# The seam between two chunks of a routed expert layer: other waits on VectorE, another order on TensorE and ScalarE

## The chip, the cores and the metric

The kernel runs on one core of a Trainium2 chip. The metric is device time in microseconds (us) of one execution; the number compared is the median of several executions. Engines are named as in the profile: PE is TensorE (PEld its weight loads), DVE is VectorE, ACT is ScalarE, POOL is GpSimd, SP is SyncE, whose queue issues most transfers.

## The reference

The input is 16 x 256 = 4096 tokens of width 128. Three residual layers follow each other: half a routed feed-forward layer, an attention without softmax over positions, and half the same feed-forward layer again.

```python
x = x + 0.5 * ffn(layernorm(x))     # first pass
x = x + attention(layernorm(x))
x = x + 0.5 * ffn(layernorm(x))     # second pass
# ffn: rmsnorm, 32 experts, 4 chosen per token
g = t @ gate_w.T + gate_b
vals, idx = top_k(g, 4); w = softmax(vals)
h1 = einsum('th,efh->tef', t, w1) + b1
h = min(h1[..., ::2], 7) * sigmoid(1.702 * glu) * (clip(h1[..., 1::2], -7, 7) + 1)
out = einsum('tef,ehf->th', h * combine, w2) + combine @ b2
```

## The kernel before, in words

The tokens are cut into two chunks of 16 tiles of 128 tokens (NCHUNK = 2, CT = 16). For each chunk a router finds four experts per token. POOL then writes the normalised rows into a DRAM array `xs[c]`, sorted by expert, with 64 indirect transfers (L539, one for each tile and choice). The sorted rows make 24 **groups** of 512 slots per chunk (NG = 24), padded so that every 128 slots have one expert. The function `experts(f)` works through the 48 groups of both chunks (NGF = 48), in the first pass (f = 0) and in the second (f = 1). SP stores what comes out to `ys[c]`, and POOL gathers it back per token with 64 indirect transfers per chunk (L564); VectorE adds the gathered rows to `X`.

For group n the steps are these, each on one engine:

- SP loads 512 rows into `xrow[n % 2]` (L356, 256 KB).
- PE turns them, `turn_rows(n)`, four transposes into a PSUM bank (L1214, from `xrow`); ACT copies the bank to `xT` (`copy_rows`, L639).
- PE makes `first_product(n)` (L1311); DVE clips its two halves (`glu`, L1005, and `lin`, L1010), ACT makes `swish` (L631), and DVE makes `hid` (L1018).
- PE turns that, `turn_hid(n)` (L1214, from `hid`), into the bank `HT`; ACT copies it to `hidT` (`copy_hid`, L634).
- PE makes `second_product(n)` into the bank `YP` (L1320); ACT copies it to `yrow` (`copy_y`, L626), and SP stores that (L361, 256 KB).

All buffers come in twos by n % 2, and `YP` and `HT` are one bank each. The engines run in software pipelines whose order is written out by hand. In step k PE does `turn_rows(k)`, `turn_hid(k-3)`, `first_product(k-1)` and `second_product(k-4)`, ACT `copy_y(k-5)`, `swish(k-2)`, `copy_hid(k-3)` and `copy_rows(k)`, and DVE `glu`, `lin` and `hid` of group k-1. An engine runs its instructions in order, so a wait holds up all that stands behind it.

**The seam** is the place where chunk 0 ends and chunk 1 begins, groups 21 to 25. The rows of group 24 can only be loaded once all 64 scatters of chunk 1 have landed (semaphore `scattered[1]`), and that is late. So PE and ACT have a function `seam()` for steps 24 to 26, in which the second products are spread out, counted by semaphores of its own (`seam_turned` for the three `turn_hid`, `seam_multiplied` for the four second products). VectorE has none: at step k it makes `hid(k-1)` after a wait for `turned >= k + 1` (L1016 and L1017), which in a usual step says that `turn_hid(k-3)` has read the buffer that `hid(k-1)` will overwrite. In the seam `turned` counts the `turn_rows` of groups 24, 25 and 26.

SP's queue around the seam, in order: store 18, wait for `scattered[1]`, load 24, load 25, stores 19 and 20, load 26, store 21, load 27, store 22, load 28, store 23 (L352 to L382). Load k waits for `turned` of step k-2. POOL's first gather of chunk 0 waits for all 24 stores of chunk 0 and, by the pacing in `keep_to_experts`, for the copy `copy_hid(24)`; from there on a gather is issued about every third of a step. The first gather of chunk 1 waits for the stores of groups 24 to 47. VectorE has one loop up to group step 27 (COMB_A = 28) and from there another, in which it also adds gathered tiles.

Of the kernel before, what the change touches and what calls it, by code (L numbers as in the profile page):

```python
# [25 lines left out]
NG = ST // GT  # L26
# [12 lines left out]
NGF = NCHUNK * NG  # L39
# [35 lines left out]
def live(k, lag, n):  # L75

    return not isinstance(k, int) or 0 <= k - lag < n
# [8 lines left out]
def build(nc, x, wq, bq, wk, bk, wvT, bv, wfqT, bfq, wfkT, bfk,  # L86
          nscale, gwT, gate_b, w12T, b1, b2, out, xs, ys):
    with ExitStack() as ctx:  # L88
# [489 lines left out]
        def _(act):  # L578
# [42 lines left out]
            def experts(f):  # L621
# [11 lines left out]
                def copy_hid(n, r):  # L633
                    a.activation(hidT[:, r, :], HT, ACT.Copy).then_inc(hidT_ready, 1)  # L634
# [19 lines left out]
                def seam():  # L654
# [9 lines left out]
                    copy_y(k - 4, 0, m - 2, YP)  # L664
                    swish_of(k - 1, 1)
                    act.wait_ge(seam_multiplied, y + 2)
                    copy_y(k - 3, 1, m - 2, YP)
                    act.wait_ge(seam_turned, z + 2)
                    copy_hid(k - 2, 0)
                    copy_rows(k, 0)  # L670
# [108 lines left out]
        def _(dve):  # L779
# [209 lines left out]
            def experts(f):  # L989
# [3 lines left out]
                def step(k, r, adding=None):  # L993
# [19 lines left out]
                    if live(k, 1, NGF):  # L1013
                        dve.wait_ge(swish_ready, k + g0)
                        dve.wait_ge(lin_ready, k + g0)
                        if live(k, 3, NGF):  # L1016
                            dve.wait_ge(turned, k + (t0 + 1))  # L1017
                        v.scalar_tensor_tensor(hid[:, s, :], lin[:, s, :], 1.0, swish[:, s, :], ALU.add, ALU.mult)\  # L1018
                            .then_inc(hid_ready, 1)
# [7 lines left out]
                for k in range(4):  # L1027
                    step(k, k % 2)
                with dve.Fori(0, (COMB_A - 4) // 4) as i:
                    for j in range(4):  # L1030
                        step(i * 4 + (4 + j), j % 2)
                with dve.Fori(0, CTA // 2) as i:
                    for j in range(4):
                        step(i * 4 + (COMB_A + j), j % 2, Combine(i * 2 + j // 2, j // 2, i, 0, f) if j % 2 else None)
# [174 lines left out]
        def _(pe):  # L1209
# [74 lines left out]
            def experts(f):  # L1284
# [50 lines left out]
                def seam():  # L1335
                    k = NG
                    turn_hid(k - 3, 1).then_inc(seam_turned, 1)
                    first_product(k - 1, 1).then_inc(multiplied, 1)
                    second_product(k - 4, 0, YP, k - 4).then_inc(seam_multiplied, 1)
                    turn_rows(k, 0, k // 2).then_inc(turned, 1)  # L1340
                    second_product(k - 3, 1, YP, k - 3).then_inc(seam_multiplied, 1)
                    turn_hid(k - 2, 0).then_inc(seam_turned, 1)
                    turn_rows(k + 1, 1, k // 2).then_inc(turned, 1)
# [181 lines left out]
```

## Time and profile before

| What | Value |
| --- | --- |
| median of 3 executions | 724.93 us (724.14 to 725.18) |
| span of the profiled execution | 722.9 us |
| PE busy | 531.0 us, 73% |
| POOL busy | 506.2 us, 70% |
| DVE busy | 436.2 us, 60% |
| ACT busy | 347.2 us, 48% |
| POOL gathers (L564) on the chain that ended last | 8% of the span |

The span runs from the first to the last instruction of the profiled execution; no time of that execution beside its span was recorded. The median of the timed executions stands 2.0 us above the span, which is what lies around the instructions, and differences between executions. The kernel's stages lie in the span so: front and first router up to about 114 us, experts of the first pass up to 291 us, attention and the second router up to 460 us, experts of the second pass up to 634 us, and the last gathers and additions up to the end. Busy shares are averages over these stages; whether a wait costs time is read from the place where it lies.

### The profile page before, as it was taken

To read this page: it belongs to the slowest core of one execution; us is meant where nothing else is said; L and a number is where in the kernel's file an instruction comes from. 1 tells how busy PE (TensorE), PEld (TensorE's weight loads), DVE (VectorE), ACT (ScalarE), POOL (GpSimd) and SP (SyncE) were. 2 spreads that over 40 slices of the span, in tenths; PEclk is the share of its full clock that TensorE was granted. 3 is DMA by queue.
4 is the path that set the end of the run, shared out by engine and by line. 5 is a ranking of instruction groups with operands and counts; after the bars stand their busy time and mean duration, and the time that the engine had idled before them with its cause. 6 is when DMAs were issued, how large, how long until landed. Compare 5 with 4: busy or idle time off the path is not lost. (4 is left out here: it accounts for less than half of the span.)

```text
span 722.9 us, 12843 instructions
## 1 busy us (share of the span) xinstructions
PE 531.0 (73%) x3252; PEld 443.8 (61%) x3253; DVE 436.2 (60%) x1243; ACT 347.2 (48%) x752; POOL 506.2 (70%) x551
## 2 busy tenths in 40 slices
PE   6258879999899999385607854999999999933000
PEld 3154366999899998253504553699998999833000
DVE  6889233555547778378993868255564767845222
ACT  4444413666556666495606644366665666610000
POOL 3677777777527777777677777777752777767765
PEclk9556999999999999797557955999999999977555
DMA  7997115566546664222111111456655666524222
GB/s 271 392 375 289 52 54 153 197 194 200 175 147 197 199 210 154 81 54 53 48 52 54 51 52 55 138 182 208 203 168 177 201 198 206 160 78 128 66 62 58
DMA packets 56493, 108.28 MB, mean 150 GB/s; under 512 B 12576, under 2 KB 19968, under 8 KB 56320
## 3 DMA queue, kind: packets, MB, share of 16 engines
q1 hardware_dynamic: 40064, 74.13, 30.7%
q0 software_dynamic: 16384, 33.59, 16.1%
q8 instruction: 23, 0.38, 0.2%
q14 instruction: 22, 0.18, 0.1%
HBM read 51.00 MB, written 56.62 MB: 149 GB/s over the span
## 5 line engine op out<-in xcount | busy, mean ns | idle before, releaser
L564 POOL DMA_INDIRECT YG<-ys,row x256 | 245.0, 957 | 116.9 <-issue 75.4
L539 POOL DMA_INDIRECT xs<-U,row x256 | 250.7, 979 | 81.9 <-issue 74.6
L1311 PE MATMUL PS<-W,xT 128*128 x768 | 182.2, 380 | 0.2
L1311 PEld LDWEIGHTS PS<-W,xT 128*128 128x128 f32 x768 | 138.4, 190 | 16.1 <-issue 1.2
L1005 DVE TENSOR_SCALAR glulin<-PS 128x512 f32<-128x512 f32 x96 | 66.3, 691 | 127.8 <-PE PS L1320 84.3
L626 ACT ACTIVATE yrow<-PS 128x512 f32<-128x512 f32 x96 | 57.3, 597 | 103.3 <-PE PS L1320 103.3
L1320 PEld LDWEIGHTS PS<-W,hidT 128*128 128x128 f32 x768 | 100.7, 193 | 7.8 <-issue 3.4
L1320 PE MATMUL PS<-W,hidT 128*128 x768 | 102.8, 277 | 1.6 <-issue 1.2
L1018 DVE SCALAR_TENSOR_TENSOR hid<-glulin,swish 128x512 f32<-128x512 f32 x96 | 66.6, 694 | 16.0 <-ACT swish L631 10.5
L631 ACT ACTIVATE swish<-glulin 128x512 f32<-128x512 f32 x96 | 60.4, 629 | 30.5 <-DVE glulin L1005 26.7
L639 ACT ACTIVATE xT<-PS 128x512 f32<-128x512 f32 x96 | 56.3, 589 | 38.8 <-PE PS L1214 38.7
L1010 DVE TENSOR_SCALAR glulin<-PS 128x512 f32<-128x512 f32 x96 | 65.3, 680 | 0.0
L1214 PE MATMUL PS<-ident,xrow 128*128 128x128 f32 x384 | 58.5, 275 | 3.9 <-DMA xrow<-xs 3.8
L1214 PE MATMUL PS<-ident,hid 128*128 128x128 f32 x384 | 58.1, 274 | 1.9 <-ACT hidT L634 1.9
L634 ACT ACTIVATE hidT<-PS 128x512 f32<-128x512 f32 x96 | 55.6, 579 | 0.9 <-PE PS L1214 0.9
L1214 PEld LDWEIGHTS PS<-ident,xrow 128*128 128x128 f32 x384 | 45.4, 142 | 7.3 <-DMA xrow<-xs 6.5
L1214 PEld LDWEIGHTS PS<-ident,hid 128*128 128x128 f32 x384 | 45.2, 141 | 2.3 <-DVE hid L1018 2.3
L1063 DVE SCALAR_TENSOR_TENSOR PS<-YG,wtop,X 128x128 f32<-128x128 f32 x40 | 12.4, 353 | 50.5 <-issue 44.5
L981 DVE SCALAR_TENSOR_TENSOR X<-YG,wtop,X (+1 forms) x96 | 32.8, 341 | 3.9 <-DMA YG<-ys,row 3.9
L1214 PE MATMUL PS<-ident,U 128*128 128x128 f32 x64 | 14.5, 386 | 24.7 <-ACT U L595 24.7
L1231 PEld LDWEIGHTS PS<-gw,xT 128*128 128x128 f32 x128 | 25.8, 296 | 6.0 <-issue 3.6
L583 ACT ACTIVATE vq<-vq 128x32 f32<-128x32 f32 x6 | 1.4, 229 | 58.2 <-DVE vq L808 58.2
(178 smaller groups left out, 714.2 us busy)
## 6 DMA issues: line engine op xcount, KB each, us to landing
xrow<-xs SPq DMA_DIRECT2D x96, 256.0 KB
ys<-yrow SPq DMA_DIRECT2D x96, 256.0 KB
xs<-YG SPq DMA_DIRECT2D x6, 2048.0 KB, 13.7
W<-in_w12T SPq DMA_DIRECT2D x1, 6144.0 KB, 33.5
xs<-U,row POOLq DMA_INDIRECT x256
YG<-ys,row POOLq DMA_INDIRECT x256, 2.5
out<-X SPq DMA_DIRECT2D x7, 256.0 KB, 2.6
X<-in_x SPq DMA_DIRECT2D x4, 256.0 KB, 3.6
```

Source lines behind the costliest of these rows:

```text
L539: pool.indirect_dma_start(out=xs[c], out_offset=bass.IndirectOffsetOnAxis(ap=row[:, i:i + 1], axis=0), in_=U[:, (c * CT + t) * H:(c * CT + ...
L564: pool.indirect_dma_start(out=YG[:, t * TOPK + k, :], out_offset=None, in_=ys[c], in_offset=bass.IndirectOffsetOnAxis(ap=row[:, i:i + 1], ...
L626: a.activation(yrow[:, r, :], bank, ACT.Copy).then_inc(yrow_ready, 1)
L631: a.activation(swish[:, r, :], glu[:, r, :], ACT.Gelu_apprx_sigmoid).then_inc(swish_ready, 1)
L634: a.activation(hidT[:, r, :], HT, ACT.Copy).then_inc(hidT_ready, 1)
L639: a.activation(xT[:, r, :], TP[r], ACT.Copy, bias=1.0).then_inc(xT_ready, 1)
L1005: v.tensor_scalar(glu[:, s, :].rearrange("p (q f) -> p q f", q=GT), h1[:, 0], LIMIT, None, ALU.min).then_inc(glu_ready, 1)
L1010: v.tensor_scalar(lin[:, s, :].rearrange("p (q f) -> p q f", q=GT), h1[:, 1], -LIMIT, LIMIT, ALU.max, ALU.min).then_inc(lin_ready, 1)
L1018: v.scalar_tensor_tensor(hid[:, s, :], lin[:, s, :], 1.0, swish[:, s, :], ALU.add, ALU.mult)\
L1214: last = te.transpose(dst[:, q * P:(q + 1) * P], src[:, q * H:(q + 1) * H], ident[:])
L1311: last = te.matmul(h1, xT[:, r, q * P:(q + 1) * P], W[:, bass.ds(es[q], 2 * H)], start=True, stop=True)
L1320: last = te.matmul(bank[:, q * H:(q + 1) * H], hidT[:, r, q * P:(q + 1) * P], W[:, bass.ds(es[q] + 2 * H, H)], start=True, stop=True)
```

## The change

It has three parts. First, in PE's `seam()` the instructions `turn_hid(22)` and `second_product(21)` stand before `turn_rows(24)`; before, `turn_rows(24)` stood first, then `second_product(21)` and `turn_hid(22)`. Second, in ACT's `seam()` `copy_hid(22)` stands before `copy_y(21)`. Third, VectorE's `hid` of groups 23, 24 and 25 waits for `seam_turned` (1, 2 and 3 in its pass), which counts `turn_hid(21)`, `turn_hid(22)` and `turn_hid(23)`, and no longer for `turned`. For that VectorE's loop ends at step 23, and steps 24 to 27 are written out. Nothing is added or left out of the computation, and POOL and SP have the same instructions in the same order.

```diff
--- before.py
+++ after.py
@@ -663,10 +663,10 @@
                     act.wait_ge(seam_multiplied, y + 1)
                     copy_y(k - 4, 0, m - 2, YP)
                     swish_of(k - 1, 1)
+                    act.wait_ge(seam_turned, z + 2)
+                    copy_hid(k - 2, 0)
                     act.wait_ge(seam_multiplied, y + 2)
                     copy_y(k - 3, 1, m - 2, YP)
-                    act.wait_ge(seam_turned, z + 2)
-                    copy_hid(k - 2, 0)
                     copy_rows(k, 0)
                     copy_rows(k + 1, 1)
                     act.wait_ge(seam_multiplied, y + 3)
@@ -1013,7 +1013,9 @@
                     if live(k, 1, NGF):
                         dve.wait_ge(swish_ready, k + g0)
                         dve.wait_ge(lin_ready, k + g0)
-                        if live(k, 3, NGF):
+                        if isinstance(k, int) and NG <= k < NG + 3:
+                            dve.wait_ge(seam_turned, 3 * f + k - NG + 1)
+                        elif live(k, 3, NGF):
                             dve.wait_ge(turned, k + (t0 + 1))
                         v.scalar_tensor_tensor(hid[:, s, :], lin[:, s, :], 1.0, swish[:, s, :], ALU.add, ALU.mult)\
                             .then_inc(hid_ready, 1)
@@ -1026,9 +1028,11 @@
                 dve.wait_ge(base_done, CT * (f * NCHUNK + 1))
                 for k in range(4):
                     step(k, k % 2)
-                with dve.Fori(0, (COMB_A - 4) // 4) as i:
+                with dve.Fori(0, (NG - 4) // 4) as i:
                     for j in range(4):
                         step(i * 4 + (4 + j), j % 2)
+                for k in range(NG, COMB_A):
+                    step(k, k % 2)
                 with dve.Fori(0, CTA // 2) as i:
                     for j in range(4):
                         step(i * 4 + (COMB_A + j), j % 2, Combine(i * 2 + j // 2, j // 2, i, 0, f) if j % 2 else None)
@@ -1337,9 +1341,9 @@
                     turn_hid(k - 3, 1).then_inc(seam_turned, 1)
                     first_product(k - 1, 1).then_inc(multiplied, 1)
                     second_product(k - 4, 0, YP, k - 4).then_inc(seam_multiplied, 1)
+                    turn_hid(k - 2, 0).then_inc(seam_turned, 1)
+                    second_product(k - 3, 1, YP, k - 3).then_inc(seam_multiplied, 1)
                     turn_rows(k, 0, k // 2).then_inc(turned, 1)
-                    second_product(k - 3, 1, YP, k - 3).then_inc(seam_multiplied, 1)
-                    turn_hid(k - 2, 0).then_inc(seam_turned, 1)
                     turn_rows(k + 1, 1, k // 2).then_inc(turned, 1)
                     second_product(k - 2, 0, YP, k - 2).then_inc(seam_multiplied, 1)
                     turn_hid(k - 1, 1).then_inc(seam_turned, 1)
```

PE in the first pass's seam, from the end of `second_product(20)` on (`ident,xrow` is `turn_rows`, `ident,hid` is `turn_hid`, `W,hidT` a second product, whose four matmuls are four rows, of which the first stands; L1320 before is L1324 now). Before:

```order
L1214 MATMUL PS<-ident,xrow 128x128 [waits xT_ready,xrow_loaded0]
L1214 MATMUL PS<-ident,xrow 128x128 x3
L1289 TENSOR_LOAD eid
L1320 ISA [waits yrow_ready,hidT_ready]
L1320 MATMUL PS<-W,hidT 128x128
...
L1214 MATMUL PS<-ident,hid 128x128 [waits hidT_ready,hid_ready]
L1214 MATMUL PS<-ident,hid 128x128 x3
L1214 MATMUL PS<-ident,xrow 128x128 [waits xT_ready,xrow_loaded1]
L1214 MATMUL PS<-ident,xrow 128x128 x3
```

The same place in the change:

```order
L1218 MATMUL PS<-ident,hid 128x128 [waits hidT_ready,hid_ready]
L1218 MATMUL PS<-ident,hid 128x128 x3
L1293 TENSOR_LOAD eid
L1324 ISA [waits yrow_ready,hidT_ready]
L1324 MATMUL PS<-W,hidT 128x128
...
L1218 MATMUL PS<-ident,xrow 128x128 [waits xT_ready,xrow_loaded0]
L1218 MATMUL PS<-ident,xrow 128x128 x3
L1218 MATMUL PS<-ident,xrow 128x128 [waits xT_ready,xrow_loaded1]
L1218 MATMUL PS<-ident,xrow 128x128 x3
```

The two turns of chunk 1's rows now stand together behind the work of chunk 0; what follows them (`second_product(22)`, `turn_hid(23)`, `first_product(24)`) is as before.

VectorE at the end of its first loop, in the change (L1005 is `glu`, L1010 `lin`, L1020 `hid`):

```order
L1031 COMPARE_AND_BRANCH
L1005 TENSOR_SCALAR glulin<-PS 128x512 [waits swish_ready,multiplied]
L1010 TENSOR_SCALAR glulin<-PS 128x512 [waits hid_ready]
L1020 SCALAR_TENSOR_TENSOR hid<-glulin,swish 128x512 [waits seam_turned,lin_ready,swish_ready]
...
L1020 SCALAR_TENSOR_TENSOR hid<-glulin,swish 128x512 [waits turned,lin_ready,swish_ready]
L1036 UNCONDITIONAL_BRANCH
```

Before, these four steps were the last turn of the loop, and each `hid` waited for `turned`. Now three of them wait for `seam_turned`, and the fourth for `turned` as it did.

## Rows read from the trace of the kernel before

**Rows 1.** The waits of POOL: line waited for: us in total, times, longest us

```profile
POOL YG L564 <- issue: 75.4, 229, 2.2
POOL xs L539 <- issue: 74.6, 232, 4.2
```

**Rows 2.** POOL's timeline: start, duration, instruction, [idle before <- releaser]

```profile
210.94 0.97 POOL L564 DMA_INDIRECT YG<-ys,row  x1 [17.62 <-ACT hidT L634]
...
293.47 0.94 POOL L564 DMA_INDIRECT YG<-ys,row  x1 [1.02 <-issue]
...
554.38 0.97 POOL L564 DMA_INDIRECT YG<-ys,row  x1 [16.22 <-DMA ys<-yrow]
...
636.69 0.94 POOL L564 DMA_INDIRECT YG<-ys,row  x1 [1.57 <-issue]
```

**Rows 3.** One usual step of TensorE, from the timeline of all engines

```profile
184.47 1.05 PE L1320 MATMUL PS<-W,hidT 128*128 x8
...
185.36 0.60 PE L1214 MATMUL PS<-ident,xrow 128*128 128x128 f32 x4
...
186.24 1.89 PE L1311 MATMUL PS<-W,xT 128*128 x8
```

**Rows 4.** The first pass's seam, from the timeline of all engines

```profile
194.51 1.05 PE L1320 MATMUL PS<-W,hidT 128*128 x8
...
195.48 1.09 SPq L361 DMA_DIRECT2D ys<-yrow  x2
...
195.60 0.60 ACT L626 ACTIVATE yrow<-PS 128x512 f32<-128x512 f32 x1 [1.22 <-PE PS L1320]
...
197.36 0.65 PE L1214 MATMUL PS<-ident,xrow 128*128 128x128 f32 x4 [1.79 <-DMA xrow<-xs]
...
198.05 0.69 DVE L1018 SCALAR_TENSOR_TENSOR hid<-glulin,swish 128x512 f32<-128x512 f32 x1 [1.96 <-PE PS L1214]
...
203.25 1.89 PE L1311 MATMUL PS<-W,xT 128*128 x8
...
209.50 0.58 ACT L634 ACTIVATE hidT<-PS 128x512 f32<-128x512 f32 x1
```

**Rows 5.** The second pass's seam, from the timeline of all engines

```profile
540.32 2.45 SPq L361 DMA_DIRECT2D ys<-yrow  x2
...
540.71 1.05 PE L1320 MATMUL PS<-W,hidT 128*128 x8
...
541.80 0.60 ACT L626 ACTIVATE yrow<-PS 128x512 f32<-128x512 f32 x1 [1.22 <-PE PS L1320]
...
542.27 0.66 PE L1214 MATMUL PS<-ident,xrow 128*128 128x128 f32 x4 [0.51 <-DMA xrow<-xs]
...
542.88 1.15 PE L1320 MATMUL PS<-W,hidT 128*128 x8
...
546.72 1.89 PE L1311 MATMUL PS<-W,xT 128*128 x8
```

**Rows 6.** Windows: stretch, length, PE, PEld, DVE, ACT, POOL busy, PEclk, DMA, GB/s

```profile
194.00:196.00 2.00, 1.57 (x12) 1.30 (x10) 1.89 (x3) 0.78 (x2) 0.00 (x0) 1.00 0.31 40
196.00:197.36 1.36, 0.00 (x1) 0.00 (x1) 0.09 (x1) 0.72 (x2) 0.00 (x0) 1.00 0.84 283
197.36:198.50 1.14, 0.90 (x6) 0.66 (x7) 0.45 (x1) 0.00 (x0) 0.00 (x0) 1.00 1.03 395
198.50:200.00 1.50, 1.50 (x11) 1.50 (x11) 0.24 (x1) 0.25 (x1) 0.00 (x0) 0.65 0.80 197
200.00:201.50 1.50, 1.50 (x8) 1.18 (x6) 0.00 (x0) 1.24 (x3) 0.00 (x0) 0.50 0.39 150
```

**Rows 7.** Windows, the second pass's seam, columns as above

```profile
543.80:545.00 1.20, 1.10 (x11) 0.86 (x9) 0.00 (x0) 0.94 (x2) 0.00 (x0) 1.00 0.90 222
```

**Rows 8.** The page's DMA issues, median us to landing last

```profile
out<-X SPq DMA_DIRECT2D x7, 256.0 KB, 2.6
```

**Rows 9.** VectorE where it enters its next loop, from the timeline

```profile
214.63 0.69 DVE L1005 TENSOR_SCALAR glulin<-PS 128x512 f32<-128x512 f32 x1 [1.41 <-PE PS L1320]
```

## The prediction

> **What bounds the kernel now.** I read the waits first, for the engine that never rests. POOL waited 229 and 232 times for nothing but its own issue before a gather or a scatter, and nearly all these waits are of 0.3 us [rows 1]: it sends transfer after transfer. POOL's timeline then shows where it does rest [rows 2]. In each pass it waits once for long, between the last scatter of chunk 1 and the first gather of chunk 0: 17.62 us up to 210.94, and 16.22 us up to 554.38. From 210.94 the chain is tight up to the next long wait (64 gathers bring it to 293.47, where it waits 1.02 us instead of 0.3 for the last stores; then gathers and scatters of the attention stage), and from 554.38 up to 636.69, where the wait is 1.57 us, again for the last stores. So the kernel's length is POOL's chain plus two rests, and each rest ends with the experts' work on PE, ACT and DVE. What ends the first rest is the copy of `hid` 24, which starts at 209.50 and takes 0.58 us [rows 4]: 0.86 us later the gather starts. Store 23 comes at nearly the same time. Both lie some steps behind `first_product(24)`, so the question is when that product starts.
>
> The timeline of the two seams answers it. In the first pass PE ends `second_product(20)` at 195.56, has nothing for 1.79 us until the rows of chunk 1 are in (197.36), and only then goes on with work of chunk 0 that needed no rows [rows 4]. `hid` 23 on DVE sits 1.96 us in the same wait and starts at 198.05. `first_product(24)` starts at 203.25. In the second pass the rows are in at 542.27, PE had waited 0.51 us, and the product starts at 546.72 [rows 5]: 4.45 us after the rows against 5.89 us in the first. The windows tell why: in the first pass the granted clock is 0.65 and then 0.50, that is the 1.2 GHz level, from about 199 us on, behind PE's idle 1.79 us [rows 6]; in the second, with shorter idle times, it is 1.00 [rows 7].
>
> **The change part by part.** No instruction is added or dropped; the sum is about starts. The spacings on PE are those of a usual step [rows 3]: a turn starts 0.89 us after a second product does, and two turns take 0.88 us, so 0.44 each.
>
> First pass. `turn_hid(22)` starts at 194.51 + 0.89 = 195.40, since `hid` 22 is long made. `second_product(21)` must wait until ACT has emptied the bank YP: copy of y 20 from 195.60 to 196.20 [rows 4], so it starts at about 196.33 and ends at 197.38. Both turns of rows then start at 197.36 and 197.80; the rows' arrival is not changed, as SP's and POOL's orders stay. ACT has copied `hid` 22 by 197.3. Next it must copy y 21, and here is **the next wait**: the buffer `yrow[1]` is free only when store 19 has landed, and behind this copy on ACT stand both `copy_rows`, on PE `second_product(22)`. Store 19 was issued at 195.48 as third of four transfers of 262 KB. The windows moved 80, 385 and 450 KB up to 196, 197.36 and 198.5 [rows 6]; the third transfer ends at 786 KB, so at 197.36 + 321/395 = 198.17, and with some 0.2 us for its notice, an estimate, it is free at 198.4. ACT copies until 199.0, `second_product(22)` starts at 199.1, `turn_hid(23)` at 200.0 and `first_product(24)` at 200.45. ACT copies the rows of group 24 by about 199.6, so they are not late, and `hid` 23, made by 197.6 behind its `swish`, isn't either. That is 203.25 - 200.45 = **2.8 us earlier**, of which some 1.4 us is the clock, taken as kept: PE's idle pieces are now 0.33 and about 0.7 us, and pieces of 0.51 us and less went with 1.00 in the second pass. The bounds of the landing: an `out` store of the same size lands 2.6 us after issue [rows 8], 198.1, which gives 3.1 us; if it doesn't bind at all, PE's spacing gives 3.7; a landing at 199.2 gives 2.0. I take 2.8 because the four transfers share the queue, which the `out` stores don't.
> The Trainium skill ("DMA: Bandwidth & Descriptors", section "Anatomy of one DMA") gives a DMA, measured there on GpSimd's path, as 2.0 us plus its bytes at 436 GB/s. That makes 2.6 us here, as the `out` row does, and the gain would be 3.1 us by it.
>
> Second pass. `second_product(21)` waits for the copy of y 20, over at 542.40 [rows 5], and starts at 542.48. The turns follow at 543.37 and 543.81. That is 1.1 us later than the first turn before; what hangs on it, load 26, has over 3 us until PE wants it. Store 19, issued at 540.32, is in at 543.2 by the 2.9 us of above, before y 21 is ready (543.53). Then `second_product(22)` starts at 544.25, `turn_hid(23)` at 545.14, `first_product(24)` at 545.58, against 546.72: 1.14 us. A second product behind idle time took 0.61 us to start instead of 0.44 [rows 5], so I take **1.05 us**, with 0.5 to 1.2 as bounds.
>
> What ends the rests follows: behind `first_product(24)` all stands as before, so the copy of `hid` 24 and store 23 move by the same amounts, and POOL's two chains with them. The last stores of each pass come as much earlier, as PE's steady steps aren't touched; both sides of the waits at 293.47 and 636.69 move together. Attention and router start from these and move as a block. VectorE's unrolled steps cost nothing: the same twelve operations, and their cover is DVE's idle time of over 1 us a step. The sum is 2.8 + 1.05 = 3.85 us. Against the profiled execution it is 722.9 - 3.85 = 719.05 of span; with the 2.0 us that the median stands above the span, 724.93 - 3.85 = **721.1 us**.
>
> **The rivals.** My forecast (A) has 0.66.
> B, *the clock falls all the same* in the first seam, behind the two smaller idle pieces: half speed costs at least 1.5 x 0.35 + 1.5 x 0.5 = 1.3 us by the two windows [rows 6], so 1.4 + 1.05 remain, 722.5 us. For it: PE is still not full there. Against it: the second pass. 0.12.
> C, *ACT is the new bound*: stores 19 and 20 land after 199.5 since the queue is full at 395 GB/s, and ACT, standing in order, holds the rows' copies. The first gain falls to about 1.7 us and the second to 0.6: 722.6 us. 0.08.
> D, *no change*: POOL's first gather hangs on something that the product doesn't move, such as a store behind loads on SP, and only some tenths pass through: 724.3 us. The row at 554.38 names a store's landing as its releaser, which speaks for it; that store too waits for `turn_rows(26)` and y 23, which move. 0.09.
> E, *slower*: VectorE's code. It now leaves its loop right in the seam and enters the next from straight code; if its instructions aren't there, DVE stands at one such place in each pass. The trace's longest wait named issue before a repeated transfer is 4.2 us, the next 2.2 [rows 1]; at 4.2 on the path of each pass the kernel ends at 721.1 + 8.4 = 729.5 us. It decides from 1.9 us per pass on. Against it: before, VectorE entered its next loop at 214.63 with 1.41 us idle, all of it named as waiting for PE [rows 9], and at the new exit `hid` 23 has 2.4 us to spare. 0.05.
> The Trainium skill ("Runtime: NRT & Kernel Launch", section "Instruction fetch mechanics") says that a taken branch whose target is not in the two pages at hand stalls until it is fetched. The trace shows no such stall on VectorE at its present loop entry.
>
> **How the numbers follow.** About 0.2%, 1.45 us, is what a measurement of this kernel can tell from no change. A, B and C lie beyond it: faster 0.86. D is within: same 0.09. E: slower 0.05. The range runs from A with a store that doesn't bind (a gain of 3.7 + 1.2 and some tenths of scatter: 719.8) up to B and C with as much scatter, 722.9; it leaves out D, E and the edges.
>
> **What would show it.** In the changed profile: `turn_hid(22)` some 2 us before the first turn of chunk 1's rows; `hid` 23 at about 196.9, no longer released by PE; the rows still turned at about 197.4; the copy of y 21 on ACT with a wait for a DMA; `first_product(24)` near 200.4 and a clock of 1.00 from 198.5 to 203; the first gather near 208.1, and POOL's rests at 14.8 and 15.2 us instead of 17.6 and 16.2. I am wrong if the gathers don't start earlier although the product does, if the wait at 293.47 or 636.69 grows by what the first gather gained, or if the clock is 0.50 in the seam.

## The result, and the profile after

The change is slower: 725.25 us against 723.48 us (22 executions of each), ratio 1.0022 with a 95% interval of 1.0015 to 1.0029, 1.8 us by the medians, where 3.85 us less (721.1 us) were forecast. The profiled execution went from 722.9 to 724.9 us of span.

GpSimd's timeline, the changed kernel, the rows that answer to [rows 2] (start, duration, instruction, idle before and its releaser):

```profile
208.98 0.98 POOL L564 DMA_INDIRECT YG<-ys,row  x1 [15.61 <-ACT hidT L634]
...
291.54 0.95 POOL L564 DMA_INDIRECT YG<-ys,row  x1 [1.17 <-issue]
...
556.10 0.97 POOL L564 DMA_INDIRECT YG<-ys,row  x1 [17.16 <-ACT hidT L634]
...
638.71 0.94 POOL L564 DMA_INDIRECT YG<-ys,row  x1 [1.87 <-issue]
```

The first gather comes 1.96 us earlier, and at 291.54 POOL is still 1.93 us ahead of [rows 2]. At 556.10 it is 1.72 us behind, at 638.71 it is 2.02 us behind, and that is the end's difference. So the first seam gained, and between 291 and 556 us 3.65 us were lost.

**The first seam**, from the timeline of the changed kernel (L1324 is the second product, L1315 the first, L1218 the turns), beside [rows 4]:

```profile
195.53 2.35 SPq L361 DMA_DIRECT2D ys<-yrow  x2
...
195.82 1.05 PE L1324 MATMUL PS<-W,hidT 128*128 x8
...
197.76 1.15 PE L1324 MATMUL PS<-W,hidT 128*128 x8 [0.44 <-ACT yrow L626]
...
198.06 0.69 DVE L1020 SCALAR_TENSOR_TENSOR hid<-glulin,swish 128x512 f32<-128x512 f32 x1 [0.75 <-ACT swish L631]
...
198.75 1.04 PE L1218 MATMUL PS<-ident,xrow 128*128 128x128 f32 x8
199.01 0.60 ACT L626 ACTIVATE yrow<-PS 128x512 f32<-128x512 f32 x1 [0.49 <-DMA ys<-yrow]
...
201.28 1.89 PE L1315 MATMUL PS<-W,xT 128*128 x8
```

Each step is the forecast one. PE goes through chunk 0's work without waiting for rows, `hid` 23 waits for its `swish` and no longer for PE, ACT waits 0.49 us for store 19, and the granted clock stays at 1.00, the 2.4 GHz level (windows from 194.0 to 201.5). The product comes 1.97 us earlier than at 203.25, not 2.8. Two things hold ACT's copy of `y` 21 back to the same moment, and either alone would have done it. Store 19, issued at 195.53, lets the copy start only at 199.01, 3.48 us later, where the forecast took 2.9. And PE reaches the seam 1.3 us later in this execution (195.82 against 194.51), so that `y` 21 itself was ready at about 198.95 (an estimate: the copy of `y` 22 starts 1.19 us after its product does). PE's lateness began at the first turn of the pass, at 115.18 against 114.09, ahead of anything that the change touches.

**The second seam**, same view, beside [rows 5]:

```profile
540.90 1.15 PE L1324 MATMUL PS<-W,hidT 128*128 x8 [0.44 <-ACT yrow L626]
...
541.10 0.90 SPq L361 DMA_DIRECT2D ys<-yrow  x2
...
542.89 0.66 PE L1218 MATMUL PS<-ident,xrow 128*128 128x128 f32 x4 [0.84 <-DMA xrow<-xs]
...
544.70 0.60 ACT L626 ACTIVATE yrow<-PS 128x512 f32<-128x512 f32 x1 [3.04 <-DMA ys<-yrow]
...
545.54 2.07 PE L1324 MATMUL PS<-W,hidT 128*128 x8 [0.90 <-ACT yrow L626]
...
548.25 2.08 PE L1315 MATMUL PS<-W,xT 128*128 x8
```

Here the change's own order puts `second_product(21)` at 540.90. By the same 1.19 us `y` 21 was ready at about 542.1, but ACT may copy it only when store 19, issued at 541.10 behind the loads, has landed: it idles 3.04 us before 544.70, some 2.6 of them with `y` 21 ready. The store took 3.6 us. PE stands behind ACT and its clock falls, as the windows of the changed kernel show (columns as in [rows 6]):

```profile
543.00:544.50 1.50, 1.07 (x8) 0.73 (x8) 0.00 (x0) 0.00 (x0) 0.00 (x0) 1.00 1.01 388
544.50:546.00 1.50, 0.60 (x4) 0.47 (x3) 0.00 (x0) 1.30 (x3) 0.00 (x0) 0.74 0.69 209
546.00:548.00 2.00, 2.00 (x11) 2.00 (x11) 0.00 (x0) 0.63 (x2) 0.00 (x0) 0.50 0.84 252
```

**The scatters between the seams.** The 64 scatters of chunk 1 in the second pass began 1.57 us earlier than before (454.79 against 456.36) and ended 0.78 us later (538.94 against 538.16). They took 2.35 us more, in a stretch in which POOL's program is unchanged. The page's groups of the changed kernel say which transfer it was; before, the mean of L539 was 979 ns:

```profile
L564 POOL DMA_INDIRECT YG<-ys,row x256 | 245.1, 958 | 116.2 <-issue 74.9
L539 POOL DMA_INDIRECT xs<-U,row x256 | 253.2, 989 | 81.8 <-issue 74.5
```

A mean of 989 ns hides two kinds: nearly all scatters take 0.96 us, and 8 of these 64 take 1.27 to 1.46 us. Before, 2 of the 64 were so long. That is the sum: 1.57 us ahead, less 2.35 us of long scatters, less 0.94 us of a longer rest (17.16 against 16.22 us) is 1.72 us behind.

**When a scatter is long.** The changed kernel's timeline, one long scatter, and one of the kernel before:

```profile
500.13 0.69 DVE L1020 SCALAR_TENSOR_TENSOR hid<-glulin,swish 128x512 f32<-128x512 f32 x1 [0.18 <-ACT swish L631]
500.26 1.39 POOL L539 DMA_INDIRECT xs<-U,row  x1 [0.30 <-issue]
```

```profile
505.38 0.96 POOL L539 DMA_INDIRECT xs<-U,row  x1 [0.30 <-issue]
505.40 0.70 DVE L1018 SCALAR_TENSOR_TENSOR hid<-glulin,swish 128x512 f32<-128x512 f32 x1
```

VectorE's `hid` just ahead of the scatter makes it long; just behind, it does nothing, and `hid` itself takes 0.69 us in both. Take all scatters of the experts' stages in nine traces with `lin` in SBUF (the two above and `r1`, `r2`, `n`, `e7`, `e5`, `e8b` and `e9b` below) and the `hid` before each. Where `hid` started 0.05 to 0.40 us before the scatter, 109 of 110 were held (1.17 to 1.48 us, the longest where `hid` started last); the one exception, 0.96 us, lies at the edge of 0.05. Where it started 0.4 to 0.6 us before, the mean was 1.02 us. Everywhere else all took 0.95 to 0.97 us. However late the scatter starts in that stretch, it ends some 1.52 us after `hid` started, about 0.83 us after `hid` ended.

The gathers are held in the same way, though there are fewer meetings: in the nine traces 67 of 67 gathers that began 0.05 to 0.40 us after a `hid` took 1.11 to 1.44 us instead of 0.94. One of them, from the change:

```profile
213.93 0.69 DVE L1020 SCALAR_TENSOR_TENSOR hid<-glulin,swish 128x512 f32<-128x512 f32 x1 [0.19 <-ACT swish L631]
214.02 1.42 POOL L564 DMA_INDIRECT YG<-ys,row  x1 [0.30 <-issue]
```

The Trainium skill ("SBUF — State Buffer", section "Who interferes with whom") says that a VectorE operation with two inputs in SBUF contends with GpSimd operations that read SBUF, for a shared pair of ports that one holds for its whole instruction, and that issue order decides who waits. The traces agree for the transfer that starts second, at 0.45 us an encounter. They do not for `hid`, which takes 0.68 to 0.73 us in all 656 cases where it starts during a transfer of POOL. The same section infers that such an operation leaves the making of a DMA's descriptors alone; these indirect transfers are held all the same, and which part of them is held no run here shows.

### The profile page after: what moved, and what is told of

Same layout as the page of the kernel before. It is cut to its first block and busy times, and to the rows that moved or that the text cites. A ratio compares the mean times of both kernels' runs of the same rounds, so it can differ in the third digit from the quotient of the medians.

```text
span 724.9 us, 12826 instructions
## 1 busy us (share of the span) xinstructions
PE 533.5 (74%) x3252; PEld 446.9 (62%) x3253; DVE 436.2 (60%) x1243; ACT 347.6 (48%) x752; POOL 508.9 (70%) x551
## 3 DMA queue, kind: packets, MB, share of 16 engines
q0 software_dynamic: 16384, 33.59, 16.4%
## 5 line engine op out<-in xcount | busy, mean ns | idle before, releaser
L539 POOL DMA_INDIRECT xs<-U,row x256 | 253.2, 989 | 81.8 <-issue 74.5
L1315 PE MATMUL PS<-W,xT 128*128 x768 | 182.4, 380 | 0.1
L1315 PEld LDWEIGHTS PS<-W,xT 128*128 128x128 f32 x768 | 138.7, 191 | 16.0 <-issue 1.0
L1005 DVE TENSOR_SCALAR glulin<-PS 128x512 f32<-128x512 f32 x96 | 66.4, 691 | 130.7 <-PE PS L1324 84.4
L1324 PEld LDWEIGHTS PS<-W,hidT 128*128 128x128 f32 x768 | 100.8, 193 | 9.0 <-issue 4.6
L1324 PE MATMUL PS<-W,hidT 128*128 x768 | 102.9, 277 | 2.8 <-ACT yrow L626 1.8
L1020 DVE SCALAR_TENSOR_TENSOR hid<-glulin,swish 128x512 f32<-128x512 f32 x96 | 66.6, 694 | 14.8 <-ACT swish L631 11.9
L1010 DVE TENSOR_SCALAR glulin<-PS 128x512 f32<-128x512 f32 x96 | 65.4, 681 | 0.0
L1218 PE MATMUL PS<-ident,xrow 128*128 128x128 f32 x384 | 57.9, 274 | 4.1 <-DMA xrow<-xs 4.0
L1218 PE MATMUL PS<-ident,hid 128*128 128x128 f32 x384 | 58.1, 274 | 2.0 <-ACT hidT L634 2.0
L1218 PEld LDWEIGHTS PS<-ident,xrow 128*128 128x128 f32 x384 | 45.0, 141 | 7.6 <-DMA xrow<-xs 6.8
L1218 PEld LDWEIGHTS PS<-ident,hid 128*128 128x128 f32 x384 | 45.2, 141 | 2.3 <-DVE hid L1020 2.3
L1218 PE MATMUL PS<-ident,U 128*128 128x128 f32 x64 | 14.6, 388 | 24.6 <-ACT U L595 24.6
L1235 PEld LDWEIGHTS PS<-gw,xT 128*128 128x128 f32 x128 | 27.5, 313 | 6.1 <-issue 3.7
L1235 PE MATMUL PS<-gw,xT 128*128 128x32 f32 x128 | 27.5, 376 | 4.0 <-DVE topi L845 3.0
```

What stands on the lines that cost most here:

```text
L539: pool.indirect_dma_start(out=xs[c], out_offset=bass.IndirectOffsetOnAxis(ap=row[:, i:i + 1], axis=0), in_=U[:, (c * CT + t) * H:(c * CT + ...
L1005: v.tensor_scalar(glu[:, s, :].rearrange("p (q f) -> p q f", q=GT), h1[:, 0], LIMIT, None, ALU.min).then_inc(glu_ready, 1)
L1010: v.tensor_scalar(lin[:, s, :].rearrange("p (q f) -> p q f", q=GT), h1[:, 1], -LIMIT, LIMIT, ALU.max, ALU.min).then_inc(lin_ready, 1)
L1218: last = te.transpose(dst[:, q * P:(q + 1) * P], src[:, q * H:(q + 1) * H], ident[:])
L1315: last = te.matmul(h1, xT[:, r, q * P:(q + 1) * P], W[:, bass.ds(es[q], 2 * H)], start=True, stop=True)
L1324: last = te.matmul(bank[:, q * H:(q + 1) * H], hidT[:, r, q * P:(q + 1) * P], W[:, bass.ds(es[q] + 2 * H, H)], start=True, stop=True)
```

## The experiments

The theory at the start had two parts. *Held scatters*: `hid` with two SBUF inputs holds a scatter, and the change moved VectorE so that more of them meet. *Store 19*: behind the loads on SP's queue it makes ACT the bound of the new seam. The rivals: the order itself does not pay; VectorE's straight-line steps cost time where they stand; or nothing but variation between executions is seen. In the expectations the two parts together are theory 1, VectorE's written-out code is theory 2, and the order on PE and ACT is theory 3; theory 1b, of the last experiments, is that the place of VectorE's loop in its program decides how many scatters are held.

All in one table. "Rest" is the time from the end of the last scatter to the first gather, which is what the seam's order can change; "long" counts scatters over 1.2 us among the last 64 before each seam, first and second pass.

| Kernel | long | rests, us | span | median (before beside it) | ratio, 95% |
| --- | --- | --- | --- | --- | --- |
| before | 8, 2 | 17.6, 16.2 | 722.9 | 723.48 | |
| the change | 7, 8 | 15.6, 17.2 | 724.9 | 725.25 (723.48) | 1.0022, 1.0015 to 1.0029 |
| r1 before again | 7, 2 | 17.5, 16.4 | 722.3 | 723.83 (723.44) | 1.0002, 0.9988 to 1.0016 |
| r2 change again | 7, 8 | 15.7, 15.8 | 722.4 | 724.21 (723.44) | 1.0009, 0.9994 to 1.0024 |
| n before, other idle | 7, 2 | 16.1, 16.4 | 722.2 | 724.77 (723.44) | 1.0018, 0.9999 to 1.0037 |
| e7 before + store 19 | 6, 2 | 16.1, 16.4 | 721.5 | 723.31 (723.44) | 1.0002, 0.9987 to 1.0018 |
| e5 change + store 19 | 8, 7 | 14.4, 14.9 | 721.5 | 723.05 (723.66) | 0.9990, 0.9978 to 1.0003 |
| e3b change, lin in PSUM | 0, 0 | 17.9, 18.3 | 721.0 | 721.58 (723.66) | 0.9967, 0.9953 to 0.9981 |
| e4b before, lin in PSUM | 0, 0 | 18.3, 17.0 | 719.2 | 720.32 (723.66) | 0.9955, 0.9938 to 0.9972 |
| e6 change, both edits | 0, 0 | 17.9, 16.6 | 719.4 | 720.99 (723.66) | 0.9967, 0.9955 to 0.9980 |
| e8b before, VectorE moved | 7, 10 | 16.1, 17.9 | 726.5 | 729.01 (725.02) | 1.0061, 1.0039 to 1.0083 |
| e9b order + store 19 | 8, 2 | 15.0, 15.7 | 719.6 | 721.55 (725.02) | 0.9962, 0.9941 to 0.9983 |

### The parts of the change, and lin in PSUM, first try

`e1` is before with VectorE's part alone (the second and third hunk of the diff), `e2` the change with VectorE's code as before, `e3` and `e4` the change and before with `lin` kept in PSUM, so that `hid` has one input in SBUF:

```diff
-v.tensor_scalar(lin[:, s, :].rearrange("p (q f) -> p q f", q=GT), h1[:, 1],
+v.tensor_scalar(h1[:, 1], h1[:, 1],
...
-v.scalar_tensor_tensor(hid[:, s, :], lin[:, s, :], 1.0, swish[:, s, :], ALU.add, ALU.mult)\
+v.scalar_tensor_tensor(hid[:, s, :].rearrange("p (q f) -> p q f", q=GT), h1[:, 1], 1.0,
+                       swish[:, s, :].rearrange("p (q f) -> p q f", q=GT), ALU.add, ALU.mult)\
```

> The order of before on PE and ACT; only VectorE has the change (its three waits for seam_turned, its steps 24 to 27 written out). Theory 1 (the seam works, the loss is made elsewhere: scatters held up by VectorE's hid, and a late store at the second seam): the edit alone moves nothing that others wait for, since turn_hid(23) still stands behind the rows on PE; hid 23 starts about 1.2 us earlier in the first pass and no product does; time within 1 us of before, unless the meeting of scatters and hid falls out otherwise. Theory 2 (VectorE's written-out code costs the time): slower than before by about the whole 1.8 us, with idle time on VectorE at step 24 or 28 in each pass. Theory 3 (the new order on PE and ACT costs it): as before, within 0.5 us.

> The new order on PE and ACT; VectorE as before, so hid 23 waits for turn_rows(24). Theory 1: hid 23 now starts only behind the rows, about 0.7 us after turn_rows(24) starts, in time for turn_hid(23), so most of the seam's gain stays: first_product(24) about 8 to 8.5 us after the last scatter's end in the first pass (before 9.92, the change 7.90), and the total is again set by what happens to the scatters of the second pass: some 1.4 us scatters in it if it is slower than before, none if it isn't. Theory 2: as before or faster by up to 3 us, since VectorE's code is that of before. Theory 3: slower than before by 1.8 us as the change is.

> The change, and VectorE's clipped lin is written back in place in PSUM, so that hid reads one operand from PSUM and only swish from SBUF; the same values are computed. Theory 1: the scatters of about 1.4 us are gone in both passes (0 of 64, now 7 and 8), the scatters of chunk 1 take 61.5 us of POOL instead of 64.7 and 65.0, end 3 us earlier in each pass, and the kernel is faster than the change by 3 to 6 us (719 to 722 us) if PE keeps up. Theory 2 and 3 leave the long scatters unexplained: the scatters stay at 1.4 us if they are held by something else (DMA rings, SP's issues), and the time stays near 725 us.

> The kernel before, with lin in place in PSUM as in the run above. Theory 1: the 8 long scatters of the first pass and 2 of the second are gone; about 3 us off the first pass's scatter chain and 1 us off the second's, of which PE, reaching the seam at about the same time as the scatters end, lets through perhaps half: 720 to 722.5 us. Against the run above it says what the seam's change is worth where no scatter is held: theory 1 expects the change to be ahead by 2 to 4 us, theory 3 expects it behind.

In these four runs, and in four later ones, the kernel before itself took 867 to 869 us, since waits between engines were longer throughout, so nothing of some 2 us can be read from them. Why is not known. Medians 869.17, 869.68, 868.38 and 867.87 us against 869.17, ratios 1.0014, 1.0007, 1.0009 and 0.9998, all with intervals of some 0.002 or more to each side. What does hold there: with `lin` in PSUM none of the 128 scatters ahead of the seams was long, without it 2 or 3 of each 64 (1 to 4 in the later four).

### Store 19 ahead, and lin in PSUM

`e5` sends store 19 before SP waits for the scatters:

```diff
-held = {1: (NG - 5, NG - 4), 2: (NG - 3,), 3: (NG - 2,), 4: (NG - 1,)}
+held = {1: (NG - 4,), 2: (NG - 3,), 3: (NG - 2,), 4: (NG - 1,)}
...
 store(c - 1, NG - STORE_LAG, (NG - STORE_LAG) % 2)
+store(c - 1, NG - 5, (NG - 5) % 2)
 sp.wait_ge(scattered[c], 16 * PAIRS * (f + 1))
```

> The change, and SP's store of group 19 is issued before SP waits for chunk 1's scatters, no longer behind them and behind two loads. Theory 1: in both passes the copy of y 21 on ACT no longer waits for a DMA (0.49 us in the first pass of the change, 3.04 us in the second), first_product(24) starts about 7.4 to 7.9 us after the last scatter's end in both passes (7.90 and 9.31 in the change), TensorE's clock stays at 1.00 in the second seam, and the kernel is faster than the change by 1 to 2.5 us. Theory 3 (the order on PE and ACT itself costs): no more than 0.5 us faster than the change.

> The change with store 19 ahead of the wait and with lin in place in PSUM. Theory 1: no scatter of chunk 1 above 1.2 us, the scatters' end 2.5 to 3.5 us earlier in each pass on a chip where the change has 7 or 8 long ones, and no DMA wait of ACT in the seam; the fastest of all, 717 to 721 us on a chip where before takes 723 to 725. Theory 3: near 725.

> The change with lin in place in PSUM, once more, beside the two runs with store 19 ahead. Theory 1: no long scatters; against the run with both edits it shows the store's wait alone: ACT waits for store 19 in at least one seam and the time is 0.5 to 2 us above the run with both.

> The kernel before with lin in place in PSUM, once more. Theory 1: no long scatters; the rest between the last scatter and the first gather stays as long as in before or grows (17 us and more), since scatters end earlier while PE does not; 720 to 723 us where before takes 723 to 725; 1.5 to 4 us slower than the run with both edits, which is then the worth of the seam's order.

*Store 19 holds.* In `e5` ACT waits for no store in either seam, and the rests are the shortest of all, 14.4 and 14.9 us; 15 scatters are still long. The median is 0.6 us below before's, which the interval does not tell from no change.

*Held scatters hold.* With `lin` in PSUM no scatter is long in either kernel, also where `hid` comes just ahead: in the traces of `e3b`, `e4b` and `e6` 45 scatters began 0.05 to 0.40 us after a `hid`, and all took 0.95 to 0.96 us; 42 gathers did, and all took 0.94 or 0.95 us. The timeline of `e4b`, and the page's groups of `e4b` and of `e3b`:

```profile
155.59 0.69 DVE L1018 SCALAR_TENSOR_TENSOR hid<-PS,swish 128x512 f32<-128x512 f32 x1 [0.26 <-ACT swish L631]
155.69 0.96 POOL L539 DMA_INDIRECT xs<-U,row  x1 [0.30 <-issue]
```

```profile
L539 POOL DMA_INDIRECT xs<-U,row x256 | 245.8, 960 | 81.9 <-issue 78.9
```

```profile
L539 POOL DMA_INDIRECT xs<-U,row x256 | 246.5, 963 | 81.8 <-issue 76.7
```

*With the held scatters the wait for the store goes too.* In `e3b`, which leaves store 19 where it was, ACT waits for no store in either seam. This is the same copy of `y` 21 in its second seam, released by PE:

```profile
542.87 0.60 ACT L626 ACTIVATE yrow<-PS 128x512 f32<-128x512 f32 x1 [0.43 <-PE PS L1325]
```

I had expected the wait there, and `e3b` 0.5 to 2 us behind `e6`; the medians lie 0.6 us apart, and the intervals overlap.

*What missed.* I expected the change to keep a lead over before once the scatters were free, and `e6` to be the fastest. It shows none: 721.58 and 720.99 us against 720.32, with intervals that overlap. The timeline of `e4b` says why, at the first seam:

```profile
194.34 1.05 PE L1321 MATMUL PS<-W,hidT 128*128 x8
...
195.23 0.60 PE L1215 MATMUL PS<-ident,xrow 128*128 128x128 f32 x4
```

The turn of chunk 1's rows has no wait for a DMA. The scatters end 3 to 4 us earlier, so the rows are in when PE arrives, and there is nothing for the new order to go ahead of. The second seam of `e4b` has no such wait either. So the order can pay only while the rows are the last to come. The shorter edit, `lin` in PSUM alone, has the lowest ratio measured, 0.45% below before, though its interval overlaps those of `e3b`, `e6` and `e9b` below.

### Repeats, a shifted phase, and store 19 alone

`r1` and `r2` are copies of before and of the change. `n` is before with `NIDLE_E = (36, 38)` in place of `(36, 34)`, which lengthens a pause ahead of the second pass; `e7` is before with the edit of `e5`.

> The kernel before, unchanged, for a second trace of it. Theory 1 in its sharper form (where VectorE's hid falls against the scatters settles into one of two patterns; in one every third or second hid holds a scatter for 0.45 us, 7 or 8 of the 64, in the other a scatter in eleven is held for 0.1 us): the first pass has 8 long scatters again. In the second pass the pattern is that of the first trace (2 long ones) if the pattern goes with the code, and 7 or 8 in some traces if it changes from execution to execution; then before's times of 722.2 and 725.2 us are the two patterns.

> The change, unchanged, for a second trace. Theory 1: 7 or 8 long scatters in each pass; ACT waits for the store of group 19 in at least one seam, for 0.5 us or more, and up to 3 us where the scatters end late; first_product(24) 7.5 to 9.5 us after the scatters' end; the time 1 to 2.5 us above before.

> The kernel before with 38 instead of 34 idle matmuls ahead of the second pass's experts, which starts PE there about 0.6 us later against the scatters and changes nothing else. Theory 1: only the place of hid against the scatters is moved, so the second pass may settle into the other pattern; if it does, it has 7 or 8 long scatters, they end about 2.4 us later, and the time is about 2 us above before. If the pattern stays, the time is within 0.8 us of before. Theory 3 (what costs is the order of the seam) expects no more than 0.7 us either way.

> The order of before on all engines, and only store 19 ahead of the wait for the scatters. Theory 1: in before's order PE waits for the rows before second_product(21), so the copy of y 21 on ACT never waited for a store; nothing to gain, within 0.5 us of before, and SP's load 24 at most 0.1 us later. With the run of the change and this same edit (723.05 us) it says whether store 19 and the new order only pay together.

The counts of long scatters repeat: 7 and 2 in the copy of before, 7 and 8 in the copy of the change. So they seem to belong to the program and not to the execution, and another phase of PE's start (`n`) leaves them at 7 and 2. `n` was expected within 0.8 us of before; it is 1.3 us above it, with an interval that just reaches no change, and no long scatter to explain that. The copy of the change waits for store 19 again, 0.54 and 2.93 us, but its clock stays at 1.00 through the second seam, its second rest is 15.8 us, and it is only 0.8 us slower by the medians, with an interval that includes no change (1 to 2.5 us were expected). The clock's fall at 545 us is thus a matter of some executions, and so is part of the loss. Its copy of `y` 21 in the second seam:

```profile
543.73 0.60 ACT L626 ACTIVATE yrow<-PS 128x512 f32<-128x512 f32 x1 [2.93 <-DMA ys<-yrow]
```

Store 19 alone (`e7`) gives nothing that can be told: in before's order PE waits for the rows first. The first rest of one and the same order varies by 1.5 us (17.6, 17.5, 16.1), which is as much as a seam is to gain.

### Why 2 became 8: VectorE's place in its program

Before's VectorE is uneven in the second pass. PE starts a first product each 3.49 us (469.55, 473.05, 476.54, 480.03), but VectorE's `glu` does not keep that step (timeline of VectorE, before):

```profile
472.47 0.69 DVE L1005 TENSOR_SCALAR glulin<-PS 128x512 f32<-128x512 f32 x1 [1.51 <-PE PS L1320]
...
476.31 0.69 DVE L1005 TENSOR_SCALAR glulin<-PS 128x512 f32<-128x512 f32 x1 [1.76 <-PE PS L1320]
...
479.36 0.69 DVE L1005 TENSOR_SCALAR glulin<-PS 128x512 f32<-128x512 f32 x1 [0.97 <-PE PS L1320]
```

The same place in the change:

```profile
470.72 0.69 DVE L1005 TENSOR_SCALAR glulin<-PS 128x512 f32<-128x512 f32 x1 [1.51 <-PE PS L1324]
...
474.21 0.69 DVE L1005 TENSOR_SCALAR glulin<-PS 128x512 f32<-128x512 f32 x1 [1.41 <-PE PS L1324]
...
477.61 0.69 DVE L1005 TENSOR_SCALAR glulin<-PS 128x512 f32<-128x512 f32 x1 [1.32 <-PE PS L1324]
```

Before, the intervals are 3.84, 3.05, 3.49, 3.59, 3.60, 3.29: `glu` is 0.35 us late once, in the loop's first turn, and then 0.11 us late in one step of four. In the change and in the first pass of both they are 3.49, 3.40, 3.50, 3.58, over and over. The lateness costs VectorE nothing, but it moves `hid` against the scatters. A scatter comes each 1.26 us, and eight of them with one hold (8 x 1.265 + 0.45 = 10.57 us) are about three steps (10.47 us), so in an even rhythm one hold can lead to the next. That is argued from the spacings; the trace shows the row: in the change's second pass the long ones are numbers 8, 20, 28, 36, 41, 49, 57 and 62 of 64. In before's second pass they are 10 and 20, and there the row breaks off. All six traces of this speed with before's VectorE code (before, `r1`, `n`, `e7`, `e9b`, `e4b`) have the interval of 3.84 us in the second pass, and none of the six with other code there has it.

If the place of the loop in VectorE's program does that, twelve tiny instructions of no other use, ahead of the second pass, where VectorE has some 13 us of idle time, do it too; and the order with VectorE's code left alone keeps 2 long scatters:

```diff
@@ e8, on top of before
+pad = sb("pad", [P, 16])
...
 weights()
+for i in range(12):
+    v.memset(pad[:, i:i + 1], 0.0)
 experts(1)
@@ e9: the change in seam() of PE and ACT and the edit of e5, VectorE as before
```

> The kernel before, and 12 tiny fillers on VectorE ahead of the second pass's experts, where VectorE idles for 13 us; they cost nothing themselves and only move its later instructions to other places in its program. Theory 1b (the place of VectorE's loop in its program makes one step in four 0.11 us late in before, and that lateness keeps hid from holding scatters): the glu intervals of the second pass become even (3.49 and so on, no 3.84), 7 or 8 scatters of chunk 1 are long there instead of 2, and the time is 1.5 to 2.5 us above before. If the place in the program isn't it: 2 long scatters, uneven steps and the time of before.

> The new order on PE and ACT, store 19 ahead of the wait for the scatters, and VectorE's program as before, whose hid 23 waits for the rows. Theory 1b: 2 long scatters in the second pass, no DMA wait on ACT, first_product(24) 7 to 8 us after the scatters' end in both passes; the first gather near 208 and near 551.5 us; 720.5 to 722 us, 2 to 3 us ahead of before, of which the store alone gave nothing in before's order.

> Before's order on PE and ACT, VectorE's part of the change alone. Theory 1b: no gain in the seam (first_product(24) 8.5 to 10 us after the scatters' end), even steps and 7 or 8 long scatters in the second pass: 724.5 to 726 us, above before. Theory 3 (the order on PE and ACT costs the time): before's time.

> The order of PE and ACT alone, VectorE's program as before. Theory 1b: 2 long scatters in the second pass, ACT waiting for store 19 in the second seam; about 722 to 723.5 us, at or below before. Theory 3: near the change's 724 to 725 us.

Medians 866.12, 866.61, 868.30 and 865.90 us against 866.80: nothing to tell. With the longer waits of these executions the place of VectorE's code makes no difference to the second pass's long scatters either: 2, 2 and 2 with it moved (`e1`, `e1b`, `e8`), 3, 1 and 4 without (`e2`, `e2b`, `e9`). What follows holds where before takes some 724 us. The two that decide were run again, where before took 725.02 us:

> The kernel before with 12 tiny fillers on VectorE ahead of the second pass's experts, in its 13 us of idle time, once more. Theory 1b (place in the program): even glu intervals in the second pass, 7 or 8 long scatters there instead of 2, 1.5 to 2.5 us above before, on a chip where before takes 723 to 725 us. If the place isn't it: uneven steps, 2 long scatters and before's time.

> The new order on PE and ACT with store 19 ahead and before's VectorE program, once more. Theory 1b: 2 long scatters in the second pass, no DMA wait of ACT in the seam, first_product(24) 7 to 8 us after the scatters' end in both passes, first gathers near 208 and 551.5 us; 720.5 to 722 us where before takes 723 to 725.

`e8b`: the intervals become even (3.49, 3.40, 3.50, 3.58), 10 scatters of the second pass are long instead of 2, and the kernel is 4.0 us slower, more than the 1.5 to 2.5 us expected. The work of before has not changed, only where it stands. Beside the first trace of before, the second pass's scatters take 2.95 us longer and the rest behind them 1.66 us: PE waits for the rows, and the granted clock is 0.50 from 546 to 548 us. The page's group and the second seam, where PE waits:

```profile
L540 POOL DMA_INDIRECT xs<-U,row x256 | 253.5, 990 | 81.9 <-issue 73.7
```

```profile
544.54 0.66 PE L1217 MATMUL PS<-ident,xrow 128*128 128x128 f32 x4 [3.35 <-DMA xrow<-xs]
```

`e9b`: 8 and 2 long scatters, rests of 15.0 and 15.7 us, and 3.5 us faster than before. The second seam of `e9b` (lines one higher):

```profile
541.20 1.04 PE L1215 MATMUL PS<-ident,xrow 128*128 128x128 f32 x8
541.40 0.60 ACT L627 ACTIVATE yrow<-PS 128x512 f32<-128x512 f32 x1 [0.43 <-PE PS L1321]
...
541.93 0.69 DVE L1019 SCALAR_TENSOR_TENSOR hid<-glulin,swish 128x512 f32<-128x512 f32 x1 [2.08 <-PE PS L1215]
...
543.67 1.90 PE L1312 MATMUL PS<-W,xT 128*128 x8
```

ACT copies `y` 21 with no wait for a store, and the product is 3.05 us earlier than before; 2.43 of these are there because the scatters end that much earlier (535.73 against 538.16), most of it the first seam's gain. `hid` 23 still waits 2.08 us for a turn of rows and delays nothing here. So VectorE's part of the change, the only one that moved its loop, was not needed for the gain. `e5` and `e9b` differ in that part alone: with it the second pass has 7 long scatters and the ratio is 0.9990, without it 2 and 0.9962. The two were measured beside different executions of before, and their intervals overlap. `pad` may also have moved tensors allocated after it in `e8b`; nothing of that kind differs between `e5` and `e9b`.

## Why the prediction was wrong

- **The mechanism of the seam was right.** The chain was read rightly: the first gather follows `first_product(24)`, and order plus a free store 19 gave 3.5 us (`e9b`, interval 1.2 to 4.3), near the 3.85 forecast. That the sizes agree is in part luck: the first rest of before's order on PE and ACT is 17.6 and 17.5 us in two traces and 16.1 in three others (`n`, `e7`, `e8b`), and the second seam gave `e9b` only 0.5 us of rest.
- **First pass, 2.8 us: mis-sized.** 1.96 us came. The store's wait was there, and the clock held. The term that was too small is the store's landing: 2.9 us from its issue by the forecast, of which 0.2 came from no row, and 3.48 us in the trace (ACT started at 199.01, not 198.4). The forecast's own bound for a landing at 199.2, a gain of 2.0 us, was nearly met. PE's later arrival would have cost as much by itself, so the trace can't tell the two apart. From `r1` to `r2` the gain was 1.66 us (210.41 to 208.75).
- **Second pass, 1.05 us: failed at "Store 19 is in at 543.2, before y 21 is ready (543.53)".** The 2.9 us were again too few: the user of the buffer started 3.60 us after the issue, and 3.50 in `r2`. With 3.5 us from 540.32 the store is in at 543.8, behind `y` 21 even at the forecast's own times. And the forecast held the arrival of PE and the issue of the store fixed against each other. The store is issued 2.16 us after the last scatter in both traces. PE arrived 1.8 us earlier, since it kept the first seam's gain, while the scatters had lost theirs and ended 0.8 us later. Rival C's wait came in the seam where I had ruled it out, 3.04 us of ACT's idle time, and in this execution rival B's clock with it.
- **"VectorE's unrolled steps cost nothing": failed, and this is the missing term.** The same twelve operations did cost VectorE nothing. They moved the loop of the second pass out of a lag that had kept `hid` off the scatters, and 6 more of them were held: 2.35 us on the chain that sets the end. That the place decides is what `e8b` and `e9b` show; that it does so through the lag is inferred from the intervals. Rival E had the direction, slower, and the thing, the place of VectorE's code, but not the way: it looked for VectorE standing still, and instead a small lateness went away, which cost time on POOL. The row that was read against it, idle time named as waiting for PE [rows 9], could not have shown this: the late `glu` at 472.47 has PE as its releaser too.
- **"So the kernel's length is POOL's chain plus two rests": true, but I took the chain's own length as fixed.** The page of before already had the hint: a mean of 979 ns for a scatter against 957 ns for a gather, 22 ns x 256 or 5.6 us, about which I did not ask. The gathers' own 957 has held ones in it as well: with `lin` in PSUM (`e4b`) the means are 960 and 950.

Not settled: which part of the change's loss is the DVE part alone, since `e1` and `e2` were only timed where 2 us cannot be told, and the traces of the change differ by 1.4 us in the second rest, which goes with the clock; and what makes VectorE late by 0.35 and 0.11 us at one place in its program. The Trainium skill ("Runtime: NRT & Kernel Launch", section "Instruction fetch mechanics") has taken branches wait for instructions that are not at hand; `e8b` shows that the place decides, but no run here shows a fetch.

## What to carry to other kernels

Where one engine's chain of equal transfers sets the end, list their durations singly before forecasting a reorder: a mean 2% over the usual value can hide a collision that a move of another engine's phase may make more or less frequent. Take the collision away at its root first (here one operand in PSUM, 0.45%), since a shift of code that does not touch the chain can otherwise be worth as much as the change under test. And put a transfer that frees a buffer ahead of a queue's long wait, since its time and that of its user move independently.

## What the runs showed of the hardware

- An indirect scatter issued from GpSimd is held by a VectorE operation with two SBUF inputs that started 0.05 to 0.40 us before it: 1.17 to 1.48 us instead of 0.96, in 109 of 110 cases; with one input in PSUM in 0 of 45. An indirect gather is held alike, 1.11 to 1.44 us instead of 0.94 in 67 of 67 cases, and in 0 of 42. VectorE's operation is not held in return: 0.68 to 0.73 us.
- Twelve one-column writes on an idle VectorE, 13 us of slack around them, made the kernel 4.0 us slower (`e8b`): 8 more scatters held, and behind them a longer wait of TensorE for its rows.
- A 256 KB store issued behind two loads of 256 KB on SP's queue let the user of its buffer start 3.5 to 3.6 us after its issue (3.60 in the change, 3.50 in `r2`), against a median of 2.6 us for a store of that size from issue to landing [rows 8].
- TensorE behind a waiting ACT fell from a granted clock of 1.00 to 0.50 in one execution of the change, after idle pieces of 0.84, 0.43 and 0.90 us, and stayed at 1.00 in another, after pieces of 0.84, 0.35 and 0.88 us (ACT idle for 3.04 and 2.93 us).
